# Last two slots multiplied into their batches, and a reordered hand-over between the gram passes and the expert slots

## The reference, cut to what matters

```python
def gram(x):                      # per image, xf is (256, 256 positions)
    o = (xf @ xf.T) @ (W @ xf)
    return gamma * o + xf
def experts(x):                   # 2048 tokens of 256 channels
    probs = softmax(x @ gate_w.T)             # 8 experts
    rw, sel = top_k(probs, 2); rw = rw / sum(rw)
    for e in range(8):
        h = gelu(x @ w1[e].T) * (x @ w3[e].T)
        out += combine[:, e] * (h @ w2[e].T)
x = x + gram(_gn(x))
x = x + experts(_gn(x))
```

## Time and profile before

| | us |
|---|---|
| median of three runs (lowest, highest) | 618.02 (616.23, 622.52) |
| the profiled execution's own time | 620.29 |
| its span | 618.4 |
| TensorE busy | 560.0 (91%) |
| VectorE busy | 482.2 (78%) |
| ScalarE busy | 325.9 (53%) |
| GpSimd busy | 387.8 (63%) |

### The profile page before, as it was taken

The page is one execution under the profiler, slowest core; times in us unless marked ns, Lnnn a source line. Parts: engine busy times, 40 slices in busy tenths (PEclk is TensorE's granted clock), DMA queues, the critical chain, the costliest instruction groups (busy, mean ns, idle before and its releaser), DMA issues.

```text
span 618.4 us, 13013 instructions
## 1 busy us (share of the span) xinstructions
PE 560.0 (91%) x4594; PEld 350.3 (57%) x4595; DVE 482.2 (78%) x878; ACT 325.9 (53%) x703; POOL 387.8 (63%) x243
## 2 busy tenths in 40 slices
PE   3998798999999999999999999999989979999993
PEld 1554455655555555555555555688857545555662
DVE  5659877999999999999999999886675923333345
ACT  2624675677676767677676666344324423333330
POOL 2200475999999999999999999331050565656531
PEclk9999696999999999999999999999988989999997
DMA  7130437323323322332432300000122122222267
GB/s 218 36 106 1 135 118 278 100 101 98 104 76 102 106 87 88 109 89 83 108 98 78 109 2 3 1 1 1 55 79 86 32 91 88 79 79 87 82 243 229
DMA packets 34288, 56.62 MB, mean 92 GB/s; under 512 B 8541, under 2 KB 21494, under 8 KB 34102
## 3 DMA queue, kind: packets, MB, share of 16 engines
q1 hardware_dynamic: 29766, 44.74, 23.6%
q0 software_dynamic: 3744, 10.39, 5.4%
q10 hardware_dynamic: 720, 0.72, 0.4%
HBM read 38.43 MB, written 17.40 MB: 90 GB/s over the span
## 4 chain that ended last, share of the span: by engine, by line
PE 33%; DVE 31%; issue 27%; DMA 6%; ACT 2%; POOL 0%; SPq 0%; ACTq 0%; POOLq 0%; DVEq 0%
DVE m_bf L984 14%; PE ps L1789 11%; PE ps L1810 5%; DVE x_hat L991 5%; DMA k_stack<-qk_parts 2%; DVE stats L821 2%; PE ps L1778 1%; PE ps L1799 1%; PE ps L1493 1%; PE ps L1670 1%; PE ps L1742 1%; PE ps L1723 1%; PE ps L1587 1%; PE ps L1509 1%; DVE x_hat L863 1%
## 5 line engine op out<-in xcount | busy, mean ns | idle before, releaser
L452 POOL TENSOR_TENSOR e_ring<-e_ring,x_hat 128x1024 f32<-128x1024 f32 (+1 forms) x127 | 269.8, 2127 | 29.4 <-ACT x_hat L639 17.5
L629 ACT ACTIVATE e_ring<-ps 128x1024 f32<-128x1024 f32 x128 | 131.1, 1025 | 88.3 <-PE ps L1596 88.3
L984 DVE TENSOR_REDUCE m_bf<-ps 128x128 bf16<-128x1024 f32 x128 | 155.8, 1218 | 3.0 <-PE ps L1587 2.9
L991 DVE TENSOR_REDUCE x_hat<-e_ring 128x128 f32<-128x1024 f32 x128 | 155.2, 1213 | 3.1 <-ACT e_ring L629 3.1
L1587 PE MATMUL ps<-q_stack,k_stack 72*128 72x128 bf16 x1024 | 136.5, 315 | 1.7 <-DMA k_stack<-qk_parts 1.7
L1587 PEld LDWEIGHTS ps<-q_stack,k_stack 72*128 72x128 bf16 x1024 | 101.4, 131 | 28.5 <-issue 24.9
L1596 PE MATMUL ps<-m_bf,ident_neg 128*128 128x512 bf16 x256 | 79.4, 392 | 15.0 <-DVE m_bf L984 7.6
L1615 PE MATMUL ps<-e_ring,v_slot 128*32 128x128 f32 x2048 | 85.7, 284 | 1.1 <-POOL e_ring L452 0.6
L1615 PEld LDWEIGHTS ps<-e_ring,v_slot 128*32 128x32 f32 x2048 | 49.9, 109 | 56.1 <-issue 53.0
L1789 PE MATMUL ps<-w_sb,e_ring 128*128 x156 | 76.4, 614 | 1.3 <-issue 0.7
L470 POOL DMA_INDIRECT e_ring<-token_rows,slot_x x39 | 37.8, 969 | 47.9 <-DVE slot_y L1269 32.1
(11 more groups left out here) (227 smaller groups left out, 681.7 us busy)
## 6 DMA issues: line engine op xcount, KB each, us to landing
q_stack<-qk_parts SPq DMA_DIRECT2D x32, 288.0 KB
k_stack<-qk_parts SPq DMA_DIRECT2D x32, 288.0 KB
w_sb<-in_w13T_dram SPq DMA_DIRECT2D x16, 256.0 KB, 7.3
qk_parts<-e_ring SPq DMA_DIRECT2D x8, 384.0 KB, 2.9
qk_parts<-scratch SPq DMA_DIRECT2D x2, 1536.0 KB, 18.6
x_res<-in_x_dram SPq DMA_DIRECT2D x8, 256.0 KB, 4.3
w_sb<-in_w2T_dram SPq DMA_DIRECT2D x8, 256.0 KB, 7.4
work<-pair_rows SPq DMA_DIRECT2D x8, 256.0 KB, 3.3
```

What stands on the lines that cost most here:

```text
L452: nc.gpsimd.tensor_tensor(ev, ev, view(x_hat, CH + (u % RS) * P, [[0, quads], [1, P], [0, 2]]), ALU.mult).then_inc(norm_done, 1)
L629: nc.scalar.activation(e_ring[:, u % ER, :], score_banks(v), ACT.Exp).then_inc(exp_done, 1)
L984: nc.vector.tensor_reduce(m_bf[:, u % 2], by_position(score_banks(v).rearrange("p a c -> p (a c)")), AXY, ALU.max).then_inc(max_done, 1)
L991: nc.vector.tensor_reduce(s_sum[:, u % 2], by_position(e_ring[:, u % ER, :]), AXY, ALU.add).then_inc(sum_done, 1)
```

## The change

- *Kept slots.* The last two slots (37 and 38) are not scattered. Zeros go to their places in the planes instead, early. Their ring rows are multiplied on TensorE with one-hot rows (`placed_rows`) into batches 6 and 7, and VectorE adds the products to `x_res`. The planes of batches 6 and 7 so wait only for slots 0 to 36 and the zeros. (KEPT is 2, SENT 37, LAST_ROWS 33, FIRST_BATCHES 6.)
- *Rows of slots 33 to 38* are evicted by ScalarE instead of VectorE.
- *Order at the end.* TensorE's `turn_batch` calls stand between the last slots' steps, VectorE's sums and additions likewise. ScalarE asks for its planes ahead of slot 38's rows. The stores of batches 2 to 6 wait for the planes, and ScalarE's queue issues three of them.
- *Hand-over.* Statistics of batches 4 to 7 are taken one batch at a time, two of them inside the passes; the counting of slots is split from `early_experts`, which follows the variance; TensorE's wait for the experts moves from the first turned rows to the first hidden product, and the group product moves ahead of the first turned rows.
- *Gram passes.* Normalisation of chunk 0 goes behind the finished batch of pass 3, the first gate products to the end of pass 4, `token_rows` ahead of `ranks`; ScalarE evicts the turned batches 3 and 4 one pass ahead.
- *Slot plan.* The fifth gated half goes ahead of the first placing of the second half.

```diff
 @gpsimd
-            for k in range(3, SLOTS):
+            for k in range(3, SENT):
...
+                if k >= SENT - KEPT - 2 and k < SENT - 2:
+                    send_blank(k + KEPT + 2)
 @sync
-                sp.wait_ge(y_out[i], 16 * ((SLOTS - i + YR - 1) // YR))
+                sp.wait_ge(y_out[i], 16 * ((SENT - i + YR - 1) // YR))
+            sp.wait_ge(blank_out, 16 * KEPT)
...
-            for b in range(DONE_BATCHES, B):
-                store_out(b)
+            sp.wait_ge(y_in[B - 1], 16 * TOP)
+            store_out(2)
+            store_out(3)
+            store_out(B - 1)
 @scalar
-                if b != 2:
+                if b not in (2, 3, 4):
                     turned_x(b)
-                if b == 3 or b == 5:
+                if b == 5:
                     deviation(3, (b - 3) // 2)
...
-                if b == 1:
+                if b == 1 or b == 2:
                     turned_x(b + 1)
                     lower_block(b)
...
                 if b == 3:
+                    turned_x(b + 1)
+                    lower_block(b)
+                    deviation(3, 0)
                     normalise(3, 0)
...
+                if isinstance(s, int) and s - 3 >= LAST_ROWS:
+                    expert_rows(s - 3)
...
             slot_steps(act, slot_step)
+            turned_gated(SLOTS - 2, SLOTS - 2)
+            expert_rows(SLOTS - 3)
+            gelu(SLOTS - 1, SLOTS - 1)
+            expert_rows(SLOTS - 2)
+            turned_gated(SLOTS - 1, SLOTS - 1)
...
...
+            expert_rows(SLOTS - 1)
+            act.wait_ge(y_in[B - 1], 16 * TOP)
+            store_out(4)
+            store_out(5)
+            act.wait_ge(kept_added, 1)
+            store_out(6)
 @vector
+                if b == 5:
+                    batch_statistics(4)
...
+                    batch_statistics(5)
-            dve.wait_ge(x3_done, B)
-            statistics(3, 2)
-            statistics(3, 3)
+            batch_statistics(6)
+            batch_statistics(7)
+            sums_of_chunks(2)
+            count_of_slots()
+            variance(3, 2, 2)
             early_experts()
-            variance(3, 2, 2)
...
+            gated_half(4, 4)
             place_in_slot(1, 0)
...
+            nc.vector.memset(blank, 0.0).then_inc(blank_done, 1)
...
+            slot_steps(dve, slot_step, SLOTS - 1)
+            own_gate(SLOTS - 1, (SLOTS - 1) % XR)
+            sum_planes(1)
+            add_batch(0)
+            sum_planes(2)
+            gated_half(SLOTS - 2, SLOTS - 2)
+            add_batch(1)
+            for b in range(3, FIRST_BATCHES):
+                sum_planes(b)
+            gated_half(SLOTS - 1, SLOTS - 1)
+            for b in range(2, FIRST_BATCHES):
                 add_batch(b)
             for b in range(FIRST_BATCHES, B):
                 sum_planes(b)
+            add_batch(FIRST_BATCHES)
+            dve.wait_ge(x4_done, FIRST_BATCHES + 1)
             for b in range(FIRST_BATCHES, B):
-                add_batch(b)
+                add_kept(b)
+            dve.wait_ge(kept_added, B - FIRST_BATCHES)
+            add_batch(B - 1)
 @tensor
-                if b == 4 or b == 6:
-                    logits((b - 4) // 2)
-                if b == 3 or b == 5:
-                    group_norm(3, (b - 3) // 2)
+                if b == 6:
+                    logits(1)
+                if b == 5:
+                    group_norm(3, 1)
                 if b >= 1:
 ...
+                if b == 3:
+                    group_norm(3, 0)
...
-            pe.wait_ge(experts_done, 1)
+            group_norm(3, 2, 2)
             turn_rows(0, 0)
             keep_busy(0, 1)
-            group_norm(3, 2, 2)
...
+            def kept_rows(s):
+                pe.wait_ge(ye_out, s + 1)
+                pe.wait_ge(places_done, s - SENT + 1)
+                pe.wait_ge(gated_done, SLOTS)
+                for b in range(FIRST_BATCHES, B):
+                    for h in range(H):
+                        i = b - FIRST_BATCHES
+                        last = nc.tensor.matmul(ps[:, (b + 1) % 2, h * N:(h + 1) * N], y_rows[:, s % YR, h * P:(h + 1) * P],
+                                                placed_rows[:, s - SENT, i * N:(i + 1) * N], start=(s == SENT and h == 0),
+                                                stop=(s == SLOTS - 1), skip_group_check=True)
+                    if s == SLOTS - 1:
+                        last.then_inc(kept_done, 1)
-            slot_steps(pe, slot_step)
-            for b in range(B):
-                turn_batch(b)
+            slot_steps(pe, slot_step, SLOTS - 1)
+            turn_batch(0)
+            slot_step(SLOTS - 1, (SLOTS - 1) % XR, lambda k: True)
+            turn_batch(1)
+            turn_gated(SLOTS - 2, SLOTS - 2)
+            projected(SLOTS - 3, SLOTS - 3)
+            hidden(SLOTS - 1, SLOTS - 1)
+            projected(SLOTS - 2, SLOTS - 2)
+            turn_batch(2)
+            turn_gated(SLOTS - 1, SLOTS - 1)
+            turn_batch(3)
+            turn_batch(4)
+            projected(SLOTS - 1, SLOTS - 1)
+            turn_batch(5)
+            kept_rows(SENT)
+            turn_batch(FIRST_BATCHES)
+            kept_rows(SLOTS - 1)
+            turn_batch(B - 1)
```

More of the change, by code:

```diff
@@ L54, in conv_stack_kernel @@
     DONE_BATCHES = 2
+    KEPT = 2
+    SENT = SLOTS - KEPT
+    LAST_ROWS = SLOTS - 6
     NONE = 64.0
@@ L159, in conv_stack_kernel @@
             "p (s j k) -> p s j k", s=3, j=TOP * HALF)
+        placed_rows = e_ring[:, 1, :].rearrange("p (s n) -> p s n", s=KEPT)
+        blank = e_ring[:, 2, 0:C]
         XR = 8
@@ L198, in conv_stack_kernel @@
         CLASS = LATE_OWN + LATE * 2 * E
-        assert CLASS + LATE <= 4096
+        IN_TILE = CLASS + LATE
+        assert IN_TILE + KEPT * TPC <= 4096
+        assert (B - FIRST_BATCHES) * N == CH and SLOTS - FIRST_SLOTS >= KEPT
         RANKS = (7 * CH + P, 6 * CH + C)
@@ L270, in conv_stack_kernel, with slot_steps @@
         y_in = [sem(f"y_in{b}") for b in range(B)]
+        places_done, blank_done, blank_out, kept_done, kept_added = (
+            sem(n) for n in ("places_done", "blank_done", "blank_out", "kept_done", "kept_added"))
         ytr_done, x4_done, out_done = sem("ytr_done"), sem("x4_done"), sem("out_done")
-        def slot_steps(eng, step):
+        def slot_steps(eng, step, last=SLOTS):
             inside = lambda k: not isinstance(k, int) or 0 <= k < SLOTS
@@ L280, in slot_steps @@
                     step(i * XR + r, r % XR, inside)
-            for s in range(SLOTS - XR, SLOTS + 3):
+            for s in range(SLOTS - XR, last):
                 step(s, s % XR, inside)
@@ L478, in scatter, with send_blank @@
                                              ).then_inc(y_out[k % YR], 16)
+            def send_blank(k):
+                pool.wait_ge(blank_done, 1)
+                nc.gpsimd.indirect_dma_start(out=y_dram[:, :], in_=blank, in_offset=None,
+                                             out_offset=bass.IndirectOffsetOnAxis(ap=slot_y[:, k:k + 1], axis=0)
+                                             ).then_inc(blank_out, 16)
             pool.wait_ge(plan_done, 1)
@@ L759, in _ @@
             turned_rows(0, 0)
+            deviation(3, 2, 2)
             turned_rows(1, 1)
-            deviation(3, 2, 2)
             normalise(3, 2)
@@ L826, in statistics, with batch_statistics, sums_of_chunks @@
                                                op1=ALU.add).then_inc(gn_sums[k], 1)
+            def batch_statistics(b):
+                dve.wait_ge(x3_done, b + 1)
+                for h in range(H):
+                    count(nc.vector.bn_stats(stats[:, b // BPC, h * BPC + b % BPC], x_res[:, h, b * N:(b + 1) * N]))
+            def sums_of_chunks(c):
+                dve.wait_ge(dve_chain, chain[0])
+                square, mean, scaled = (view(stats, c * SPC * 6 + i, [[6, 2 * SPC], [3, 2]]) for i in range(3))
+                link(nc.vector.tensor_tensor(square, mean, mean, ALU.mult))
+                nc.vector.scalar_tensor_tensor(out=square, in0=scaled, scalar=2.0 / N, in1=square, op0=ALU.mult,
+                                               op1=ALU.add).then_inc(gn_sums[3], 2)
             def statistics_of(buf, first, width):
@@ L1247, in early_experts @@
                      nc.vector.tensor_scalar(s_view(TAKEN, [1, E]), starts(1, 0), float(EARLY), None, ALU.min))
-                link(nc.vector.tensor_reduce(expert, own, AX, ALU.add))
+                count(nc.vector.tensor_reduce(expert, own, AX, ALU.add))
+            def early_experts():
+                expert = s_view(EXPERT, [1, EARLY])
                 link(nc.vector.tensor_scalar(expert, expert, float(E - 1), None, ALU.min))
@@ L1301, in _ @@
                                                    ).then_inc(x3_done, 1)
+                if b == 3:
+                    variance(3, 0)
+                    second_half(3, 0)
                 if b == 2 or b == 4:
@@ L1412, in slot_step, with places @@
                     own_gate(s, r)
```

(11 more changed lines are left out.)

52 lines of the change are left out of this document (32 added, 20 removed).

## The result

The changed kernel takes **608.78 us** (median of 6 runs, 608.05 to 609.15) against 618.35 before (median of 6, 616.23 to 622.52). The ratio is 0.9863, with a 95% interval of 0.9833 to 0.9894: 1.4% faster, and the forecast was 607.0. The profiled execution took 608.43, with a span of 606.6.

What follows compares the result with a forecast made beforehand. TensorE was taken as busy nine tenths almost throughout, leaving the passes' hand-round and an end of two transfers in series. Front 6.5 plus end 4.5 gave 11.0 us off 618.02: 607.0 us, range 601.5 to 614.

Steps and rivals of the forecast that it cites:

- the forecast's own case: The main case, whole kernel at 602 to 611.8 us, given a chance of 0.62.
- Front: Gram passes to first gate products: reordering and fewer late statistics bring gate products 6.5 us earlier, 3.8 at worst.
- The passes: Gram passes: reordering removes TensorE's waits, ranks about 2.3 us earlier, the plan 2.55 us earlier.
- The variance: After the last statistics on VectorE: starts at 453.9 against 460.39, 6.5 us earlier, the experts following at 455.25.
- The first hidden product: TensorE's first slots: starts at 455.8, after the second gather lands at 455.3; its pair takes 3.44 us at full clock.
- Slot plan: Fifth gated half ahead of placing: between 0.7 us gained and 0.9 lost, taken as nothing.
- End: Last slots to last store: planes asked for 4.1 us earlier, two slots' rows kept; 4.5 us less in all.
- The last load: Plane loads of the last two batches: 3.2 us for the first pair, 4.1 for the last, landing at 608.0.
- Both groups of kept products: TensorE at the end: first group 605.6 to 607.3 under the loads, second 607.75 to 609.5 behind batch 6's transposes.
- the last store: After VectorE's last addition: needs 2.55 us as before; other stores done by about 612.5, under it.
- The stall: ScalarE idles 4.38 us without a shown releaser; TensorE loses 6.0 us from 496 to 508; forecast leaves it unchanged.
- ScalarE's stall vanishes: Rival: the stall in the slots disappears, whole kernel at 601.0 us; chance 0.07.

Runs made afterwards that it cites:

- the two later profiles of the old front: Profiles of the kernel before with only the new end, and with only GpSimd's transfer order altered; last score product to first gate product: 80.65 and 80.68 us.
- TensorE padded: Changed kernel with 88 idle, long-fulfilled waits ahead of all TensorE's work; they took 9.4 us, and the stall stayed at slots 8 to 10.
- all gathers held: Changed kernel, every late gather from slot 10 held until rows two slots ahead are turned, slots 8 and 14 scattered without a gather; 601.53 us, ratio 0.9725 to before.
- gathers 10-16 held: Changed kernel with only the gathers of slots 10 to 16 held until the rows two slots ahead are turned; 613.05 us.
- end only: Kernel before with only the change's new end, gram passes and statistics old; 0.5% (0.1 to 0.9) faster than before.

## Why the prediction was right

It gave 11.0 us and a range of 601.5 to 614; 9.6 came, in the forecast's own case. By its steps, the front's times counted from the last score product, the end's from slot 37's row transposes:

- **Front, 6.5 forecast, 6.0 measured.** The passes gave 2.8 for 2.55. The variance came at the time I gave, within 0.2, the experts 0.3 early. The first hidden product is 0.45 late. Slot 1's rows were there when I said (their transposes start at 455.28 on the clock of before, for 455.3), but I let the hidden product start 0.5 behind them and it starts 0.98 behind, after a filler product and 0.31 us of idling. The profile puts that idling down to ScalarE's eviction of slot 1's rows; the kernel's text asks there only for slot 0's, evicted 1.4 us before, so what held it stays open. That the clock would stay at the full level was right in every profile with the whole new front. But I had taken the lower level of the old one as given. That part, 1.7 us by the two later profiles of the old front, is a gain in some executions only.
- **Slot plan, nothing forecast, 0.5 gained** from the gate products to hidden product 7, inside the 0.7 to -0.9: the wait of 0.57 us is gone.
- **End, 4.5 forecast, 3.6 measured.** Mis-sized three times, each by a little. The planes were asked for at the time I gave. The last load took 4.4 us to land, not 4.1. The fit of the Trainium skill (DMA: Bandwidth & Descriptors, Anatomy of one DMA) was measured on transfers that GpSimd issues, and these loads are issued by SyncE and ScalarE; the estimate of 4.4 that I worked out from it agrees here. The same load took 4.1 to 5.2 in the other runs with this end. Both groups of kept products start 0.85 late, because in TensorE's queue batch 4's transposes wait 0.22 us for VectorE's addition of batch 2, and slot 38's projection restarts behind them; that sets the chain, and hides the landing. And the last store needs 2.90 us, not 2.55, with the held stores still moving beside it; with the stores free it was 2.58.
- **The stall, left as it is.** It cost 1.8 more than before, and the stretch behind it gave 1.3 back, which I have not followed up. That these two nearly cancel, where I had put nothing for either, is luck. The mechanism that I gave the stall failed: I put it down to ScalarE and to code loading. The rule that I quoted from the Trainium skill (Runtime: NRT & Kernel Launch, Instruction fetch mechanics) doesn't apply to it: the stall stayed when ScalarE's loop was written out and when ScalarE's and TensorE's streams were shifted, and it moved by six slots when only GpSimd's gathers were held. A 16 KB instruction packet, which the stall contained in the first four traces, lies ahead of the late signals in "TensorE padded" (494.9, they begin at 499.9), and at 491.2 in "all gathers held", which has no stall there. What the stall follows is a run on GpSimd, which the earlier trace rows had shown as 7.32 us busy of 12, and which I had not looked into.

Of the rivals, none happened. "ScalarE's stall vanishes", 601.0, is what the last experiment makes by hand: 601.53.

What stays open: whether TensorE's products are late or only their signals, and what in GpSimd's indirect transfers delays them. Also open is what distinguishes the nine gathers of the front. Of the four profiles in which TensorE waits for the experts in the old place, two have the full clock behind that wait and two the lower level; what decides it was not tried.

## What to carry to other kernels

When two engines idle at once and the profile can't name a releaser, compare their starts with the ends that the trace gives to the engine that both wait for: here that engine's signals were late. Then look for what another engine does without a pause at that time, and shift that. Moving a chain of transfers under an engine's work is worth the distance to that engine's own chain: here the end became TensorE's after 3.6 us. And before you compare two traces, find the last instant ahead of the change and subtract there: 2.2 of 11.8 us were not the change's.

## What the runs showed of the hardware

- While GpSimd issued nine or ten indirect transfers, scatters and gathers in turn, 1.27 to 1.32 us apart with 0.30 us between them, TensorE's signals came up to 7.0 us behind the modelled end of their products, from about 5 us after the run began until 1.7 to 1.8 us after it ended (the changed kernel, the kernel before, gathers 10-16 held). Behind five in a row a signal was 1.4 to 1.5 us late, and with pauses of 0.75 us per pair, from 493 to 502 us, none was (all gathers held). With nine gathers in a row and no scatter it was 0.7 (changed kernel).
- A wait that is long fulfilled still takes TensorE 0.107 us as an instruction of its own (88 in 9.4 us, TensorE padded).
- With the same instructions behind the same wait of 2.53 us, TensorE's granted clock over the first 3.4 us of the hidden pair was 0.63 in one execution (the kernel before) and 1.00 in another (end only).
